# Turning E right behind x, ahead of the Toeplitz products, in an S4D convolution

## The reference

```python
A = -jnp.exp(log_A_real) + 1j * A_imag
dtA = A * dt[:, None]
P = dtA[:, :, None] * jnp.arange(length, dtype=jnp.float32)
Cs = Cc * (jnp.exp(dtA) - 1.0) / A
K = 2.0 * jnp.einsum('hn,hnl->hl', Cs, jnp.exp(P)).real
...
y = jnp.fft.irfft(u_f * k_f, n=n)[..., :Lq]
y = y + u_m * D[:, None]
return y * mask[:, None, :]
...
x = x + _L0_cond_ref(x, itok_B_8_3872, L0_cond_log_dt, L0_cond_C, L0_cond_log_A_real, L0_cond_A_imag, L0_cond_D)
```

## Time and profile before

| | us |
|---|---|
| median of three runs | 859.32 |
| lowest and highest | 857.62, 860.59 |
| profiled execution, its own time | 858.43 |
| its span, first to last instruction | 856.6 |
| TensorE busy in the span | 819.1 |
| VectorE busy | 733.3 |
| GpSimd busy | 648.2 |
| ScalarE busy | 618.4 |

### The profile page before, as it was taken

One profiled execution on the slowest core, in us unless ns is written; L12 is line 12 of the kernel. 1 busy time (PEld: TensorE's weight loads), 2 busy tenths in 40 slices (PEclk: granted clock), 3 DMA queues, 4 the chain that ended last, 5 costly groups with the idle time before them and its releaser, 6 DMA issues.

```text
span 856.6 us, 22236 instructions
## 1 busy us (share of the span) xinstructions
PE 819.1 (96%) x6174; PEld 754.2 (88%) x6174; DVE 733.3 (86%) x2016; ACT 618.4 (72%) x1716; POOL 648.2 (76%) x720
## 2 busy tenths in 40 slices
PE   0689999999999999999999999999999999999997
PEld 0579989888999999999999999999999999999996
DVE  8978988888888888888888888888888888888886
ACT  3667777777777777777777777777777777777774
POOL 7897777777777777877787777778787877777761
PEclk9999999999999999999999999999999999999999
DMA  5055787777777777777877777787777777777775
GB/s 110 5 115 135 183 200 180 190 186 181 189 193 183 193 186 196 186 195 189 192 189 184 194 183 196 187 195 189 192 192 186 198 184 195 184 195 186 198 186 135
DMA packets 161367, 152.76 MB, mean 178 GB/s; under 512 B 13504, under 2 KB 161216, under 8 KB 161216
## 3 DMA queue, kind: packets, MB, share of 16 engines
q1 hardware_dynamic: 161344, 152.48, 72.2%
HBM read 84.08 MB, written 67.30 MB: 177 GB/s over the span
## 4 chain that ended last, share of the span: by engine, by line
PE 87%; DMA 4%; DVE 3%; POOL 2%; SPq 2%; issue 1%; ACT 1%; DVEq 0%; POOLq 0%; ACTq 0%
PE y L1006 13%; PE y L1008 13%; PE y L1007 13%; PE y L1043 12%; PE v L1023 10%; PE xt_even L991 6%; PE xt_odd L991 6%; DMA xall<-in_x_dram 4%; PE v L1006 3%; PE v L1007 3%; PE v L1008 3%; PE y L1001 2%; PE y L1002 2%; SPq L345 1%; DVE q L748 1%
## 5 line engine op out<-in xcount | busy, mean ns | idle before, releaser
L545 ACT ACTIVATE room<-v 64x192 f32<-64x192 f32 (+1 forms) x768 | 235.8, 307 | 170.2 <-DVE v L899 153.3
L899 DVE SCALAR_TENSOR_TENSOR v<-v,RV,mid 128x192 f32<-128x192 f32 (+2 forms) x512 | 192.4, 376 | 55.0
L899 DVE SCALAR_TENSOR_TENSOR mid<-room,RV,v 128x192 f32<-128x192 f32 (+2 forms) x512 | 184.4, 360 | 41.2 <-ACT room L545 21.9
L1006 PE MATMUL y<-thi,uhi 128*128 128x256 f32 x512 | 186.4, 364 | 0.0
L895 DVE COPY_PREDICATED xall<-mask,y 128x512 f32<-128x512 int32 x256 | 176.0, 736 | 1.4 <-issue 1.4
L1006 PE MATMUL y<-fhi,zhi 128*128 128x256 f32 x512 | 154.6, 302 | 1.8 <-DVE zlo L722 1.6
L1008 PE MATMUL y<-thi,ulo 128*128 128x256 f32 x512 | 144.5, 282 | 0.0
L1008 PE MATMUL y<-fhi,zlo 128*128 128x256 f32 x512 | 144.0, 281 | 0.0
L1007 PE MATMUL y<-tlo,uhi 128*128 128x256 f32 x512 | 144.0, 281 | 0.0
L1007 PE MATMUL y<-flo,zhi 128*128 128x256 f32 x512 | 144.0, 281 | 0.0
L524 POOL TENSOR_TENSOR room<-W,B 128x512 f32 (+1 forms) x127 | 141.9, 1117 | 0.0
(11 more groups left out here) (179 smaller groups left out, 1945.4 us busy)
## 6 DMA issues: line engine op xcount, KB each, us to landing
xall<-in_x_dram SPq DMA_DIRECT2D x256, 256.0 KB, 4.7
out_dram<-xall SPq DMA_DIRECT2D x254, 256.0 KB, 3.4
traw<-krows SPq DMA_DIRECT2D x128, 128.0 KB, 2.9
NXY<-B SPq DMA_DIRECT2D x2, 512.0 KB, 6.3
out_dram<-xall SPq DMA_DIRECT2D x4, 128.0 KB, 2.4
krows<-ksb SPq DMA_DIRECT2D x8, 1.0 KB, 2.0
krows<-ksb SPq DMA_DIRECT2D x8, 4.0 KB, 4.0
krows<-ksb SPq DMA_DIRECT2D x8, 11.0 KB, 3.8
```

The source lines that it names most:

```text
L545: return act.activation(dst, src, ACT.Copy)
L899: return dve.scalar_tensor_tensor(out=out, in0=src, scalar=RV[:, k:k + 1, h], in1=other, op0=ALU.mult, op1=ALU.add)
L1006: pe.matmul(o, a_hi, b_hi, start=start, stop=False, skip_group_check=True)
```

## The change

In TensorE's slot, `turn_e` of channel h+2 is taken from between the second and the third Toeplitz chunk of channel h and put directly behind `turn_x` of channel h+2. It thereby stands ahead of `k_rest` in slots 1 to 4 and ahead of all Toeplitz products in every slot. The other engines' code is untouched.

```diff
                 if has2 and not first:
                     turn_x(*two, 0)
                     turn_x(*two, 1)
+                if has2:
+                    turn_e(*two)
                 if isinstance(g, int) and g == 0 and 1 <= j <= 4:
                     pe.wait_ge(s_pred, 2 * j - 1)
                     k_rest(j)
...
                     for c in range(2):
                         toep_even(*here, c)
                         toep_odd(*here, c)
-                if has2 and has0:
-                    turn_e(*two)
                 if has0:
                     for c in range(2, CPH):
```

## The result

The changed kernel took 860.71 us in the median of nine runs, the kernel before 857.62 in nine runs beside it; the ratio is 1.0034, its 95% interval 1.0019 to 1.0049. So the change costs 2 to 3 us.

A forecast was written before the change was run, and what follows sets the result against it. The prediction took the long middle to be bound by TensorE's own work. Terms 0 + 0 + 0.3 + 0.03 + 0.4 gave +0.7 us; between 859.1 and 860.0 it forecast 859.6 us, range 857.2 to 862.2.

The forecast's parts named there:

- The sum: All terms over the whole kernel added up: +0.7 us for the change.
- the line to which I had given 0.11: Whole kernel: chance 0.11 of a time over 861.9 us, which counts as slower by about 0.3%, 2.6 us.
- list of signs: Changed trace: slots of 6.19 us, E directly behind x, earlier copies; another slot length in the middle would mean wrong.
- Work: TensorE, every slot: E's two transposes cost the same at both places, 0 us, with +-0.5 us over 128 slots.
- Jump slots: Slots where the loop jumps back: E's wait for the masked copies costs 0, copies coming 0.24 us earlier; upper bound 1.3.
- The meeting point: ScalarE, ordinary slots: hold at E goes, turning of odds waits for TensorE's chunk sums instead; 0 gain on the path.
- Slots 1 to 4: `k_rest` and `zlo` come 0.22 us later, so TensorE waits 0.10 us in each of four slots: +0.4 us.
- Start: Slot 0: E waits for GpSimd's `pf` with the Toeplitz products behind it; a stall only moves: +0.03 us.
- Irregular slots: Slots with a late Toeplitz row: E waits 0.6 us for the copies, partly replacing another stall; net +0.3 us.
- (A): Rival: the chain does not move up and jump slots wait 0.07 us each; 861.2 us, chance 0.15.
- (B): Rival: the chain's slack removes TensorE's stalls for late states in the middle; 858.2 us, chance 0.12.
- (C): Rival: TensorE's sequencer exposes 0.22 us of waits around E in each of 108 loop slots; 883 us, chance 0.06.

The follow-up runs named there:

- second profile of the changed kernel: The changed kernel, E directly behind x, measured again beside the kernel before: 861.69 us beside 859.57, ratio 1.0019 (1.0005 to 1.0033).
- first-only kernel: Against the kernel before, E stands directly behind x in slots 0 to 5 only: 859.43 us beside 859.57, ratio 1.0001.
- loop only: Against the kernel before, E stands directly behind x in all slots but the first six: 861.61 us beside 859.57, ratio 1.0023.
- waits-only kernel: Against the kernel before, only E's two waits go behind x; its transposes stay behind the second Toeplitz chunk: 864.21 us beside 859.57, ratio 1.0050.

## Why the prediction was right, and where it was not

The time lay in the range, and the total was small as forecast; the way to it had one term wrong, and part of the hit is luck. The sum had the change at +0.7 us; measured are +3.1 and +2.1, three to four times as much. The range was laid around a median of before of 859.32 us, from three runs; nine runs put it at 857.62. Had before stayed at 859.32, the same 3.1 us would have given 862.4, just outside. By the bound of 0.3% the first measurement, 0.34% slower, is just over the line to which I had given 0.11, and the second, 0.19%, is inside. And by the prediction's own list of signs a slot of another length in the middle meant that it was wrong: that sign came, by 13 ns.

- **Work: 0, with +-0.5 us as bounds. Wrong; it is +1.6.** 121 slots x 0.0133 us. The working took the pair's own price at both places (0.23 and 0.22 us) and assumed that the rest of the slot costs the same whatever stands ahead of it. It does not: averaged over some 100 undisturbed slots, the last ten products of a slot, which did not move, take 1.186 us before and 1.197 after, and all that stands ahead of them 5.007 and 5.009. So 12 of the 13 ns arise well behind both places of E. The error of the step was to price the pair and not the slot, from two-decimal rows of one slot where 121 slots repeat it, and to set a bound of 4 ns a slot by no row at all.
- **Jump slots: 0, for the chain moves up. Right in the number**; the chain did move up, but it may not have been needed. The copies came 0.35 us earlier, not 0.24: beside the shorter distance from `uhi` to `ehi`, ScalarE is 0.10 us earlier at `uhi` itself (503.37 in a slot that starts at 500.27, 3.10 us into it; after, 507.29 - 504.29 = 3.00). The price of 0.15 us for the semaphore, and with it the upper bound of 1.3 us, was too high for this instruction: it is 0.06, by which even unmoved copies would cost E about nothing. No kernel here moves E with the chain left where it was, so that stays worked out and not measured.
- **The meeting point moves to the chunk sums. Right**: 93 waits, 33.1 us, in place of 15.
- **Slots 1 to 4: +0.4 us. Right**, at 0.3: 0.10 us in each of slots 1 to 3 and 0.02 in slot 4 where E stands ahead of the taps' table, none where it stands behind chunk 1. The changed kernel's slots 1 to 3 are 7.18 to 7.20 us, like those of the first-only kernel.
- **Start: +0.03 us. Right only when the Toeplitz row is on time.** Then slot 0 is 6.90 us, as before: in the second profile of the changed kernel E starts at 55.57 and the products from the states at 58.14, for 55.68 and 58.14 predicted. In the first profile, that of after, it was late, and the chain is ScalarE's `thi` (which waited 0.69 us for the row), GpSimd's table, E, and four chunks behind it. Timelines of ScalarE, GpSimd and TensorE:

```profile
53.73 0.42 ACT L545 ACTIVATE thi<-traw 128x256 fp32r<-128x256 f32 x1 [0.69 <-DMA traw<-krows]
...
54.91 1.26 POOL L532 TENSOR_TENSOR pf<-room 128x512 f32<-128x512 f32 x1
...
56.22 0.33 PE L1001 MATMUL y<-ident,pf 128*128 128x128 f32 x1 [1.90 <-POOL pf L532]
...
58.74 0.36 PE L1006 MATMUL y<-fhi,zhi 128*128 128x256 f32 x1
```

The products from the states start at 58.74, 0.63 later than before. GpSimd makes the rest of the taps (`tlo`) ahead of the table `pf`, so a late row now delays E, and E everything. I had taken one execution's landing for the rule.
- **Irregular slots: +0.3 us. Right in kind, its size open.** After a late Toeplitz row in after (ScalarE, VectorE, TensorE):

```profile
463.66 0.42 ACT L545 ACTIVATE thi<-traw 128x256 fp32r<-128x256 f32 x1 [1.32 <-DMA traw<-krows]
...
468.32 0.75 DVE L895 COPY_PREDICATED xall<-mask,y 128x512 f32<-128x512 int32 x1
...
468.61 0.60 PE L991 MATMUL xt_odd<-ident,xall 128*128 128x128 f32 x4
...
469.12 0.33 PE L1001 MATMUL y<-ident,room 128*128 128x128 f32 x1
```

The copies end at 469.07, E starts at 469.12 instead of 469.05, and the slot is 0.12 us long; two or three such slots follow each other. The wait for states in them is still there when the row is very late. All stalls of the 121 slots together are 6.2 and 6.3 us in the two profiles of the changed kernel and 5.4 in loop only, for 4.3 before. That is 1 to 2 us more, of which x loads are 0 to 0.9; but executions of one kernel differ by more than 3 us, so single profiles don't size this term.
- **Sum.** 1.6 (shown) + 0.3 (slots 1 to 4) + 0 to 0.6 (start) + 0.3 (irregular, as predicted, not measured) = 2.2 to 2.8 us, against 3.1 and 2.1 between the medians of the two measurements.
- **Rivals.** (A): its extra waits did not come; how little they would have cost is said above. (B): its slack came, and the stalls did not shrink by it: 6.2 us for 4.3. (C), the sequencer: no gap at E in any undisturbed slot, and the waits-only kernel has slots of 6.193 us. There the rule that the prediction took from the Trainium skill, Perfetto Trace Analysis, "Sequencer-only Instruction", costs no time. (Of E's two moved waits only one, for `s_pf`, stands alone in the order shown; the prediction counts two. The wait for the copies is on the transposes.) Where the array has run out of work, as in the jump slots of the waits-only kernel, (C)'s cost is real: 0.09 to 0.10 us for each waiting instruction in the line, close to the 0.11 that the prediction read from VectorE.

## What to carry to other kernels

On a full engine, an order is not free even where no wait changes: measure the period of a steady loop over many passes before setting a term to zero. When a wait moves up in a queue, look at what stands directly behind it: with the work itself there it cost 0.06 us, with two more waiting instructions between 0.24, and moving the waits alone cost twice as much as moving them with their work. Ask too what the moved work releases: here it freed the chain that the wait depends on. And put work that waits for a DMA behind a piece that does not: turning x one Toeplitz chunk later hid nearly all late loads.

## What was not expected of the hardware

The length of a slot depends on the order of the same 47 matmul records alone, and by steps: 6.180, 6.187, 6.193, 6.200 and 6.207 us, 6.7 ns apart, the same in every undisturbed slot of a trace. All but 6.180, which one kernel has, were seen on at least two chips. Behind x, or ahead of it, E's pair costs two steps more than behind chunk 2. Behind chunks 1, 2 and 3 it costs one step more each time, behind chunk 4 no further one. x one chunk later saves two steps with E behind chunk 2, and one with E in a row with it. Some orders differ in the part ahead of the last ten products, as E after chunk 1 (5.001 us for 5.007, then 1.186 as before); some in those ten products, which are the same in all kernels (1.197 in the changed kernel, 1.200 with E after chunk 3). So an order can act on products that stand far behind it. What sets it was not tried.
